# The first cross attention of a decoder as a pipeline over three batches

## The chip, the cores and the metric

One core of a Trainium2 chip runs the whole kernel: two decoder layers on an input of 8 batches of 256 rows by 256 columns. The metric is device time in microseconds from start to end of one execution; the median of three runs of the kernel before is 3400.91 us (3396.31 to 3406.21). PE is TensorE, DVE VectorE, ACT ScalarE, POOL GpSimd; SP issues the DMAs.

## The reference

The decoder has six sublayers, each added to a residual stream x. Only the second is changed, a linear attention over the context (16 heads of 16 columns, batches of 256 queries and 256 keys):

```python
def _focused_feature_map(x, scale):
    x = jax.nn.relu(x) + EPS
    x = x / scale
    x_norm = jnp.linalg.norm(x, axis=-1, keepdims=True)
    xp = x ** FOCUS                      # FOCUS = 3, EPS = 1e-6
    return xp / jnp.linalg.norm(xp, axis=-1, keepdims=True) * x_norm
q = input_q @ Wq + bq                    # input_q = layernorm(x)
k = input_k @ Wk + bk                    # input_k = input_v = ctx_1024
v = input_v @ Wv + bv
q = _focused_feature_map(q, softplus(scale)); k = _focused_feature_map(k, softplus(scale))
# split in heads, then
z = 1.0 / (einsum('bhic,bhc->bhi', q, k.sum(axis=2)) + EPS)
kv = einsum('bhjc,bhjd->bhcd', k, v)
x = x + einsum('bhic,bhcd->bhid', q, kv) * z[..., None]
```

## The kernel before

The residual x (`x_all`), its normalised transpose (`xnT_all`) and an identity matrix stay in SBUF; PSUM is one tensor of 8 banks. The stages (attention, this cross attention, switch attention, attention, cross attention, experts) follow one another, each as a block of one program per engine; the block ends when all its engines have ended, and in front of each stage stands a normalisation with a block of its own (`normalise`, L135 to L198). Within a block the order of an engine's work is its program, written out by hand; engines wait for each other by semaphores that count up.

The changed stage is `linear_attention` (L716). Each engine runs a loop over the 8 batches. In one batch:

- SP (L753) waits until the projections of the batch before are done and loads the batch's normalised input and its context (L755, L756). There is one buffer of each.
- PE projects K, Q and V (L770) into banks 0, 1 and 2 (4 matmuls each; a float32 matmul shows as two records in the trace), after DVE has added the result of the batch before to the residual (`out_taken`).
- DVE adds the biases of K (L834) and Q (L836) into the tile `f`, which holds the two row tiles of Q and the two of K, takes the maximum with 0 and adds EPS (L837), multiplies by the inverse scale (L838), and adds V's bias (L842).
- ACT squares the four row tiles of `f` into `f2` with their sums in `norm2` (L804); DVE multiplies to the cube `f3` (L846); ACT squares that with its sums in `norm6` (L810); DVE takes the reciprocal (L848) and the product with `norm2` (L849), the ratio; ACT takes its root (L813); DVE scales the four row tiles of `f3` with it (L853).
- PE multiplies K by V, with a column of ones for the sum over keys, into bank 3 (L776), and transposes Q into bank 4 (L781). DVE keeps the parts within a head (L858, L859), ACT copies the transposed Q to SBUF (L815), and PE multiplies the two into banks 5 and 6 (L788).
- DVE makes `z` (L864, L865), the quotient `o` (L867), and adds it to the residual (L873).

POOL has no part in this stage. The helper `over_batches` (L100), which the first attention uses already, runs a body with three flags: whether the batch itself (new), the next (ahead) and the one before (old) exist; it is written out for the rounds -1, 0, 7 and 8, and a loop runs rounds 1 to 6. `wait` (L89) leaves a wait out when its value is a constant 0 or less. `alone` (L69) is a wait followed by an increment of a semaphore that nobody waits for.

Of the kernel before, what the change touches and what calls it, by code (L numbers as in the profile page):

```python
# [11 lines left out]
ALU = mybir.AluOpType  # L12
ACT = mybir.ActivationFunctionType
AX = mybir.AxisListType

P = 128
# [699 lines left out]
def linear_attention(nc, norm, x_all, xnT_all, ident, psum, a):  # L716

    with ExitStack() as stack:
# [18 lines left out]
        consts, own_dve, own_setup = s.sem("consts"), s.sem("own_dve"), s.sem("own_setup")  # L737
        projected, taken, features_raw = s.sem("projected"), s.sem("taken"), s.sem("features_raw")
        squared, cubed, sixth, ratio_ready, factor_ready = (
            s.sem(n) for n in ("squared", "cubed", "sixth", "ratio_ready", "factor_ready"))  # L740
        features, kv_summed, kv_ready = s.sem("features"), s.sem("kv_summed"), s.sem("kv_ready")
        q_turned, qT_ready, out_ready, out_taken = (s.sem(n) for n in ("q_turned", "qT_ready", "out_ready", "out_taken"))
        own_act = s.sem("own_act")
# [16 lines left out]
        def _(pe):  # L760
            pe.wait_ge(loaded, 16 * len(loads))
            with pe.Fori(0, B) as b:
                pe.wait_ge(x_here, b * 16 + 16)
                pe.wait_ge(ctx_here, b * 16 + 16)

                pe.wait_ge(out_taken, b)
                for n, (src, weights) in enumerate(((ctxT, wk), (xnT, wq), (ctxT, wv))):
                    for t in range(TT):
                        for c in range(CC):
                            ins = pe.matmul(psum[:, n, t * D:(t + 1) * D], src[:, c, t * P:(t + 1) * P], weights[:, c, :],  # L770
                                            start=(c == 0), stop=(c == CC - 1))
                    ins.then_inc(projected, 1)
                pe.wait_ge(features, b + 1)
                for c in range(CC):
                    for t in range(TT):
                        ins = pe.matmul(psum[:, 3, c * (P + 1):(c + 1) * (P + 1)], f3[:, TT + t, c * P:(c + 1) * P],  # L776
                                        v1[:, t, c, :], start=(t == 0), stop=(t == TT - 1))
                ins.then_inc(kv_summed, 1)
                for c in range(CC):
                    for t in range(TT):  # L780
                        ins = pe.transpose(psum[:, 4, c * T + t * P:c * T + (t + 1) * P], f3[:, t, c * P:(c + 1) * P],  # L781
                                           ident[:])
                ins.then_inc(q_turned, 1)
                pe.wait_ge(kv_ready, b + 1)
                pe.wait_ge(qT_ready, b + 1)
                for t in range(TT):
                    for c in range(CC):
                        ins = pe.matmul(psum[:, 5 + t, c * KVW:(c + 1) * KVW], qT[:, c, t * P:(t + 1) * P], kv[:, c, :],  # L788
                                        start=True, stop=True)
                ins.then_inc(out_ready, 1)  # L790

        @block.scalar
        def _(act):
# [7 lines left out]
            with act.Fori(0, B) as b:  # L801
                act.wait_ge(features_raw, b + 1)
                for i in range(2 * TT):
                    ins = act.activation(f2[:, i, :], f[:, i, :], ACT.Square, accum_out=norm2[:, i:i + 1])  # L804
                ins.then_inc(squared, 1)
                act.wait_ge(cubed, b + 1)

                act.wait_ge(squared, b + 1)
                for i in range(2 * TT):
                    ins = act.activation(f2[:, i, :], f3[:, i, :], ACT.Square, accum_out=norm6[:, i:i + 1])  # L810
                ins.then_inc(sixth, 1)
                act.wait_ge(ratio_ready, b + 1)
                act.activation(factor[:], factor[:], ACT.Sqrt).then_inc(factor_ready, 1)  # L813
                act.wait_ge(q_turned, b + 1)
                act.activation(qT[:], psum[:, 4, :].rearrange("p (c t) -> p c t", c=CC), ACT.Copy).then_inc(qT_ready, 1)  # L815

        @block.vector
        def _(dve):
# [3 lines left out]
            dve.tensor_scalar(scale_e[:], inv_scale[:], CAP, None, ALU.min).then_inc(consts, 1)  # L822
            dve.wait_ge(own_act, 2)
            step.link(dve.tensor_tensor(inv_scale[:], inv_scale[:], scale_e[:], ALU.max))
            step.link(dve.reciprocal(inv_scale[:], inv_scale[:]))
            with dve.Fori(0, B) as b:
                step = Steps(dve, own_dve, b * 9, 9)
                step.wait()

                dve.wait_ge(out_taken, b)  # L830
                dve.wait_ge(projected, b * 3 + 1)
                bias = lambda v: v[:].unsqueeze(1).to_broadcast([P, TT, D])
                tile = lambda n: psum[:, n, :].rearrange("p (t d) -> p t d", t=TT)
                step.did(dve.tensor_tensor(f[:, TT:2 * TT, :], tile(0), bias(bk), ALU.add))  # L834
                dve.wait_ge(projected, b * 3 + 2)
                step.link(dve.tensor_tensor(f[:, 0:TT, :], tile(1), bias(bq), ALU.add))  # L836
                step.link(dve.tensor_scalar(f[:], f[:], 0.0, FOCUS_EPS, ALU.max, ALU.add))  # L837
# [1334 lines left out]
```

## Time and profile before

| | us |
|---|---|
| median of three runs | 3400.91 |
| profiled execution, its time | 3403.3 |
| span of that execution | 3401.4 |
| stage: first DVE instruction (L821) | 980.54 |
| stage: last DVE instruction ends (L873) | 1167.98 |
| first DVE instruction of the next stage (L162) | 1168.34 |
| separate maximum L837, of 1024 elements | 0.694 |
| four scalings L853, together | 1.14 |
| residual sum L873, of 512 elements | 0.693 |

The page divides the span into 40 slices of 85 us and shows tenths: PE busy `6788888888655489999979999999998999968998`, granted clock of PE `8888988899766689999965999999998999968999` (10 tenths are 2.4 GHz). The changed stage lies in slices 11 to 13, counted from 0. Over the whole span PE is busy 86%, DVE 55%, ACT 48%, POOL 20%. Times of instructions are microseconds from the start of the span.

### The profile page before, as it was taken

How to read it: one execution, taken by the hardware profiler on the slowest of the kernel's cores; microseconds unless marked ns; L12 is line 12 of the kernel's file. 1: busy time of each engine (PE TensorE's matmuls, PEld its weight loads, DVE VectorE, ACT ScalarE, POOL GpSimd, SP SyncE). 2: the span in 40 equal slices, each digit the busy share in tenths (PEclk: the TensorE clock that was granted, in tenths of full speed). 3: DMA queues.
4: the chain of work that ended last, by engine and by line, in shares of the span. 5: the costliest groups of instructions: out<-in, count | busy, mean ns of one | idle time of the engine just before them, and what ended most of it. 6: DMA issues, size and time to landing. Idle time of an engine off the chain costs nothing. (4 is left out here: it accounts for less than half of the span.)

```text
span 3401.4 us, 50572 instructions
## 1 busy us (share of the span) xinstructions
PE 2926.5 (86%) x17024; PEld 2085.1 (61%) x17024; DVE 1863.0 (55%) x4064; ACT 1617.8 (48%) x2895; POOL 685.0 (20%) x798
## 2 busy tenths in 40 slices
PE   6788888888655489999979999999998999968998
PEld 3344444444334356776732888888886777747887
DVE  4777877787633456656531444444444544544444
ACT  3887888878721234444511333333333555532221
POOL 1122222222100044444500000000001655620000
PEclk8888988899766689999965999999998999968999
DMA  2000000000010110110110000000002000010000
GB/s 94 4 4 3 3 0 3 3 3 0 1 35 19 54 44 23 23 42 22 21 58 0 4 3 3 3 3 3 3 0 85 4 6 6 3 69 22 6 6 28
DMA packets 88230, 60.88 MB, mean 18 GB/s; under 512 B 54816, under 2 KB 76704, under 8 KB 87648
## 3 DMA queue, kind: packets, MB, share of 16 engines
q1 hardware_dynamic: 88160, 59.99, 5.8%
q8 instruction: 39, 0.64, 0.1%
q14 instruction: 31, 0.25, 0.0%
HBM read 41.10 MB, written 8.39 MB: 15 GB/s over the span
## 5 line engine op out<-in xcount | busy, mean ns | idle before, releaser
L1772 POOL TENSOR_SCALAR x_weights<-x_weights,x_sums 128x256 f32<-128x256 f32 x256 | 231.7, 924 | 1066.5 <-DVE x_sums L1809 1066.5
L670 DVE SCALAR_TENSOR_TENSOR a_w<-a_w,a_sinks 128x384 f32<-128x384 f32 x512 | 332.7, 714 | 31.5 <-ACT a_w L505 31.5
L1074 POOL TENSOR_SCALAR f_weights<-f_weights,f_sums 128x256 f32<-128x256 f32 x256 | 232.2, 924 | 271.2 <-DVE f_sums L1304 271.2
L1501 ACT ACTIVATE a_weights<-psum,a_negmax 128x1024 f32<-128x1024 f32 x128 | 142.5, 1114 | 293.1 <-DVE a_negmax L1541 293.1
L484 ACT ACTIVATE a_e<-psum 128x1024 f32<-128x1024 f32 x192 | 195.4, 1018 | 158.0 <-PE psum L343 118.9
L1475 PE MATMUL psum<-a_v,a_turned_w 128*128 128x128 f32 x2048 | 248.3, 275 | 0.0
L1475 PEld LDWEIGHTS psum<-a_v,a_turned_w 128*128 128x128 f32 x2048 | 238.1, 192 | 0.0
L1541 DVE TENSOR_REDUCE a_negmax<-psum 128x1 f32<-128x1024 f32 x128 | 156.7, 1224 | 124.9 <-PE psum L123 124.0
L1232 ACT ACTIVATE f_weights<-psum,f_negmax 128x256 f32<-128x256 f32 x256 | 117.8, 472 | 215.1 <-DVE f_negmax L1298 215.1
L340 PE MATMUL psum<-a_qT,a_kT_half 32*128 32x512 f32 x512 | 166.5, 730 | 60.6 <-DVE a_w L685 48.7
L685 DVE SCALAR_TENSOR_TENSOR a_w<-a_e,psum 128x512 f32<-128x512 f32 x256 | 162.6, 675 | 96.1 <-ACT a_e L486 86.6
L486 ACT ACTIVATE a_e<-a_e 128x1024 f32<-128x1024 f32 x192 | 202.9, 1057 | 6.1
L1742 ACT ACTIVATE x_weights<-x_masked_s,x_negmax 128x256 f32<-128x256 f32 x256 | 126.9, 496 | 147.1 <-DVE x_negmax L1805 147.0
L505 ACT ACTIVATE a_w<-a_w 128x1536 f32<-128x1536 f32 x128 | 179.4, 1472 | 0.4
L1466 PE MATMUL psum<-all_ident,a_weights 128*128 128x128 f32 x1024 | 133.8, 274 | 9.5 <-ACT a_weights L1501 9.5
L1466 PEld LDWEIGHTS psum<-all_ident,a_weights 128*128 128x128 f32 x1024 | 118.3, 140 | 29.9 <-ACT a_weights L1501 14.2
L370 PE MATMUL psum<-a_w,a_v 128*32 128x512 f32 (+1 forms) x1024 | 114.6, 575 | 19.8 <-DVE a_w L670 19.8
L188 PE MATMUL psum<-all_ident,ln_xn 128*128 128x128 f32 x192 | 53.4, 434 | 82.3 <-DVE ln_xn L177 82.3
L121 PE MATMUL psum<-a_kT_hi,a_qT_hi 128*128 128x512 f32 x256 | 110.7, 432 | 11.3 <-DVE a_qT_lo L1535 11.3
L340 PEld LDWEIGHTS psum<-a_qT,a_kT_half 32*128 32x128 f32 x512 | 44.1, 210 | 113.5 <-DVE a_w L685 59.8
L343 PEld LDWEIGHTS psum<-a_future,a_ident_r 128*128 128x128 f32 x256 | 42.5, 209 | 113.5 <-issue 113.5
L566 POOL TENSOR_TENSOR a_ctxn<-a_ctx,a_vnull 128x256 f32<-128x256 f32 x64 | 45.1, 725 | 330.2 <-DVE a_ctx L640 330.2
(304 smaller groups left out, 6820.1 us busy)
## 6 DMA issues: line engine op xcount, KB each, us to landing
a_xnT<-all_xnT_all SPq DMA_DIRECT2D x16, 256.0 KB, 2.3
x_ctxT<-in_x_ctxT SPq DMA_DIRECT2D x16, 256.0 KB, 2.7
f_xnT<-all_xnT_all SPq DMA_DIRECT2D x16, 256.0 KB, 2.3
f_pv_rows<-f_pv SPq DMA_DIRECT2D x8, 512.0 KB, 3.1
f_pv_groups<-f_pv_rows SPq DMA_DIRECT2D x8, 512.0 KB
f_w<-in_f_w SPq DMA_DIRECT2D x2, 2048.0 KB, 10.3
all_x_all<-in_x SPq DMA_DIRECT2D x1, 2048.0 KB, 8.4
a_wq<-in_a_wq SPq DMA_DIRECT2D x2, 1024.0 KB, 9.2
```

The costliest lines, as they stand in the source:

```text
L340: pe.matmul(psum[:, 2 * x + h, :], kT_half[rows[h], step % 2, g, 0:P], qT[rows[h], g, 2 * x:2 * x + 2, :], start=True, stop=False)
L484: act.activation(e[:, x, :], psS[x], ACT.Exp).then_inc(exp_done, 1)
L486: act.activation(e[:, x, :], e[:, x, :], ACT.Ln, bias=1.0).then_inc(ln_done, 1)
L505: act.activation(wu, wu, ACT.Silu, scale=SILU_SCALE).then_inc(silu_done, 1)
L670: ins = dve.scalar_tensor_tensor(part, part, sinks[:, col:col + 1], part, ALU.is_ge, ALU.mult)
L685: ins = dve.scalar_tensor_tensor(wu[:, h, 2 * x:2 * x + 2, 0:T], by_branch(e[:, x, :]), CAP, by_branch(psS[x]), ALU.min, ALU.max)
L1074: ins = pool.tensor_scalar(w, w, sums[:, k, h, t:t + 1], None, ALU.mult)
L1466: ins = pe.transpose(psum[:, 4 + half, j * P:(j + 1) * P], weights[k % 2][:, lo:lo + P], ident[:])
L1475: ins = pe.matmul(psum[:, 6 + k % 2, 0:AD], turned_w[:, k % 2, j * P:(j + 1) * P], v[:, j, h * AD:(h + 1) * AD], start=(j == 0), stop=(j = ...
L1501: act.activation(weights[k % 2][:], psum[:, 2 * (k % 2):2 * (k % 2) + 2, :].rearrange("p a n -> p (a n)"), ACT.Exp, bias=negmax[:, k:k + 1 ...
L1541: dve.tensor_reduce(negmax[:, k:k + 1], psum[:, 2 * (k % 2):2 * (k % 2) + 2, :].rearrange("p a n -> p (a n)"), AX.X, ALU.max, negate=True) ...
L1772: ins = pool.tensor_scalar(w, w, sums[:, k, h, t:t + 1], None, ALU.mult)
```

## The change

The stage becomes a pipeline by `over_batches`. In round b, PE first projects batch b+1 and then does the KV product, the transposes and the output of batch b. DVE makes the cube of batch b, then `z` and `o` of batch b-1, K's bias of b+1, the ratio of b, Q's bias and the features of b+1, the masked KV of b, the copy of the transposed Q of b (which ACT did), and V's bias of b+1. ACT takes the sixth powers and the root of b, scales the four row tiles of b (which DVE did), K first, with a semaphore for K and one for Q, and squares the features of b+1. POOL adds `o` of batch b-1 to the residual (which DVE did). EPS is added to the biases once in the setup, and maximum and inverse scale become one instruction. SP's program is unchanged; no buffer is added. The diff from PE's program on; lines taken out are left out here, they stand in the function above:

```diff
...
         @block.tensor
         def _(pe):
             pe.wait_ge(loaded, 16 * len(loads))
...
+            def project(b):
                 pe.wait_ge(x_here, b * 16 + 16)
                 pe.wait_ge(ctx_here, b * 16 + 16)
...
+                wait(pe, features_raw, b)
                 for n, (src, weights) in enumerate(((ctxT, wk), (xnT, wq), (ctxT, wv))):
+                    if n == 2:
+                        wait(pe, v_taken, b)
                     for t in range(TT):
                         for c in range(CC):
                             ins = pe.matmul(psum[:, n, t * D:(t + 1) * D], src[:, c, t * P:(t + 1) * P], weights[:, c, :],
                                             start=(c == 0), stop=(c == CC - 1))
                     ins.then_inc(projected, 1)
...
+            def body(b, new, ahead, old):
+                if ahead:
+                    project(b + 1)
+                if new:
+                    pe.wait_ge(k_scaled, b + 1)
+                    pe.wait_ge(v_taken, b + 1)
+                    wait(pe, kv_ready, b)
+                    for c in range(CC):
+                        for t in range(TT):
+                            ins = pe.matmul(psum[:, 3, c * (P + 1):(c + 1) * (P + 1)], f3[:, TT + t, c * P:(c + 1) * P],
+                                            v1[:, t, c, :], start=(t == 0), stop=(t == TT - 1))
+                    ins.then_inc(kv_summed, 1)
+                    pe.wait_ge(q_scaled, b + 1)
+                    wait(pe, qT_ready, b)
+                    for c in range(CC):
+                        for t in range(TT):
+                            ins = pe.transpose(psum[:, 4, c * T + t * P:c * T + (t + 1) * P], f3[:, t, c * P:(c + 1) * P],
+                                               ident[:])
+                    ins.then_inc(q_turned, 1)
+                    pe.wait_ge(kv_ready, b + 1)
+                    pe.wait_ge(qT_ready, b + 1)
+                    wait(pe, o_made, b)
                     for t in range(TT):
...
+                        for c in range(CC):
+                            ins = pe.matmul(psum[:, 5 + t, c * KVW:(c + 1) * KVW], qT[:, c, t * P:(t + 1) * P], kv[:, c, :],
+                                            start=True, stop=True)
+                    ins.then_inc(out_ready, 1)
+            over_batches(pe, body)
         @block.scalar
         def _(act):
...
             step.link(act.activation(scale_e[:], scale_e[:], ACT.Exp))
             step.link(act.activation(scale_e[:], scale_e[:], ACT.Ln, bias=1.0))
             act.preload_act_table_set("sqrt_and_others")
...
+            def body(b, new, ahead, old):
+                if new:
+                    act.wait_ge(squared, b + 1)
+                    act.wait_ge(cubed, b + 1)
+                    for i in range(2 * TT):
+                        ins = act.activation(f2[:, i, :], f3[:, i, :], ACT.Square, accum_out=norm6[:, i:i + 1])
+                    ins.then_inc(sixth, 1)
+                    act.wait_ge(ratio_ready, b + 1)
+                    act.activation(factor[:], factor[:], ACT.Sqrt).then_inc(factor_ready, 1)
+                    act.wait_ge(factor_ready, b + 1)
+                    for i, done in ((TT, None), (TT + 1, k_scaled), (0, None), (1, q_scaled)):
+                        ins = act.activation(f3[:, i, :], f3[:, i, :], ACT.Copy, scale=factor[:, i:i + 1])
+                        if done:
+                            ins.then_inc(done, 1)
+                if ahead:
+                    act.wait_ge(features_raw, b + 2)
+                    for i in range(2 * TT):
+                        ins = act.activation(f2[:, i, :], f[:, i, :], ACT.Square, accum_out=norm2[:, i:i + 1])
+                    ins.then_inc(squared, 1)
+            over_batches(act, body)
+        @block.gpsimd
+        def _(pool):
+            def body(b, new, ahead, old):
+                if old:
+                    alone(pool, o_made, b, passed)
+                    x_b = x_all[:, bass.ds((b - 1) * TT, TT), :]
+                    pool.tensor_tensor(x_b, x_b, o[:], ALU.add).then_inc(x_added, 1)
+            over_batches(pool, body)
         @block.vector
         def _(dve):
...
             step = Steps(dve, own_setup)
             step.did(dve.memset(v1[:, :, :, P:P + 1], 1.0))
             dve.tensor_scalar(scale_e[:], inv_scale[:], CAP, None, ALU.min).then_inc(consts, 1)
+            step.did(dve.tensor_scalar(bk[:], bk[:], FOCUS_EPS, None, ALU.add))
+            step.did(dve.tensor_scalar(bq[:], bq[:], FOCUS_EPS, None, ALU.add))
             dve.wait_ge(own_act, 2)
             step.link(dve.tensor_tensor(inv_scale[:], inv_scale[:], scale_e[:], ALU.max))
             step.link(dve.reciprocal(inv_scale[:], inv_scale[:]))
...
+            bias = lambda v: v[:].unsqueeze(1).to_broadcast([P, TT, D])
+            tile = lambda n: psum[:, n, :].rearrange("p (t d) -> p t d", t=TT)
+            def body(b, new, ahead, old):
+                if new:
+                    dve.wait_ge(squared, b + 1)
+                    wait(dve, q_turned, b)
+                    dve.tensor_tensor(f3[:], f2[:], f[:], ALU.mult).then_inc(cubed, 1)
+                if old:
+                    dve.wait_ge(out_ready, b)
+                    outs = psum[:, 5:5 + TT, 0:CC * KVW].rearrange("p t (c n) -> p t c n", c=CC)
+                    dve.tensor_scalar(z[:], outs[:, :, :, P:KVW], FOCUS_EPS, None, ALU.add).then_inc(z_made, 1)
+                    dve.wait_ge(z_made, b)
+                    dve.reciprocal(z[:], z[:]).then_inc(z_inverted, 1)
+                    dve.wait_ge(z_inverted, b)
+                    wait(dve, x_added, b - 1)
+                    for t in range(TT):
+                        ins = dve.tensor_tensor(o[:, t, :].rearrange("p (c h d) -> p c h d", c=CC, h=HEADS_IN_CHUNK),
+                                                outs[:, t, :, 0:P].rearrange("p c (h d) -> p c h d", h=HEADS_IN_CHUNK),
+                                                z[:, t].unsqueeze(3).to_broadcast([P, CC, HEADS_IN_CHUNK, P // HEADS_IN_CHUNK]),
+                                                ALU.mult)
+                    ins.then_inc(o_made, 1)
+                if ahead:
+                    wait(dve, cubed, b + 1)
+                    dve.wait_ge(projected, b * 3 + 4)
+                    dve.tensor_tensor(f[:, TT:2 * TT, :], tile(0), bias(bk), ALU.add).then_inc(raw_f, 1)
+                if new:
+                    dve.wait_ge(sixth, b + 1)
+                    dve.reciprocal(factor[:], norm6[:]).then_inc(inverted, 1)
+                    dve.wait_ge(inverted, b + 1)
+                    dve.tensor_tensor(factor[:], factor[:], norm2[:], ALU.mult).then_inc(ratio_ready, 1)
+                if ahead:
+                    dve.wait_ge(projected, b * 3 + 5)
+                    dve.tensor_tensor(f[:, 0:TT, :], tile(1), bias(bq), ALU.add).then_inc(raw_f, 1)
+                    dve.wait_ge(raw_f, b * 2 + 4)
+                    dve.scalar_tensor_tensor(f[:], f[:], FOCUS_EPS, inv_scale[:].unsqueeze(1).to_broadcast([P, 2 * TT, D]),
+                                             ALU.max, ALU.mult).then_inc(features_raw, 1)
+                if new:
+                    dve.wait_ge(kv_summed, b + 1)
+                    wait(dve, out_ready, b)
+                    for c in range(CC):
+                        lo = c * (P + 1)
+                        dve.tensor_tensor(kv[:, c, 0:P], psum[:, 3, lo:lo + P], same_head[:], ALU.mult)
+                        ins = dve.tensor_tensor(kv[:, c, P:KVW], psum[:, 3, lo + P:lo + P + 1].to_broadcast([P, HEADS_IN_CHUNK]),
+                                                head_mask[:], ALU.mult)
+                    ins.then_inc(kv_ready, 1)
+                    dve.wait_ge(q_turned, b + 1)
+                    dve.tensor_copy(qT[:], psum[:, 4, :].rearrange("p (c t) -> p c t", c=CC)).then_inc(qT_ready, 1)
+                if ahead:
+                    dve.wait_ge(projected, b * 3 + 6)
+                    for t in range(TT):
+                        ins = dve.tensor_tensor(v1[:, t, :, 0:P], psum[:, 2, t * D:(t + 1) * D].rearrange("p (c d) -> p c d", c=CC),
+                                                bv[:].rearrange("p (c d) -> p c d", c=CC), ALU.add)
+                    ins.then_inc(v_taken, 1)
+            over_batches(dve, body)
```

## Rows read from the trace of the kernel before

**Rows 1.** Busy time by stretch: its length, then each engine's, clock, DMA share, GB/s
```profile
core 0: us, PE busy (x) PEld busy (x) DVE busy (x) ACT busy (x) POOL busy (x), PEclk, DMA share, GB/s
980.54:1167.98 187.44, 97.75 (x352) 80.09 (x352) 76.83 (x180) 37.09 (x148) 0.00 (x0) 0.68 0.07 22
...
1053.15:1076.00 22.85, 12.07 (x44) 10.00 (x45) 9.29 (x22) 4.21 (x18) 0.00 (x0) 0.65 0.08 23
1260.00:1500.00 240.00, 224.58 (x1790) 163.79 (x1791) 147.73 (x225) 112.08 (x321) 112.27 (x124) 1.00 0.12 29
1800.00:1850.00 50.00, 50.00 (x51) 12.48 (x50) 5.53 (x8) 4.78 (x8) 0.00 (x0) 0.50 0.00 0
```
**Rows 2.** Waits, 980 to 1168: who for whom, us in total, times, longest
```profile
ACT x_f L804 <- DVE x_f L838: 97.9, 8, 13.5
```
**Rows 3.** Timeline, 1053 to 1076: start, us, engine, line; in brackets idle time before
```profile
1053.15 3.53 PE L770 MATMUL psum<-x_wk,x_ctxT 128*128 128x256 f32 x8 [2.40 <-DVE all_x_all L873]
1056.52 1.89 PE L770 MATMUL psum<-x_wq,x_xnT 128*128 128x256 f32 x8
1058.25 1.89 PE L770 MATMUL psum<-x_wv,x_ctxT 128*128 128x256 f32 x8
...
1060.27 0.50 SPq L755 DMA_DIRECT2D x_xnT<-all_xnT_all  x1
1060.97 0.43 SPq L756 DMA_DIRECT2D x_ctxT<-in_x_ctxT  x1
...
1061.16 0.42 ACT L804 ACTIVATE x_f<-x_f 128x256 f32<-128x256 f32 x1 [11.71 <-DVE x_f L838]
...
1067.73 2.09 PE L776 MATMUL psum<-x_v,x_f 128*128 128x129 f32 x8 [7.59 <-DVE x_f L853]
...
1069.61 1.06 PE L781 MATMUL psum<-all_ident,x_f 128*128 128x128 f32 x4
...
1075.16 0.69 DVE L873 TENSOR_TENSOR all_x_all<-all_x_all,x_o 128x512 f32 x1 [0.15 <-DVE x_o L867]
...
1076.00 3.75 PE L770 MATMUL psum<-x_wk,x_ctxT 128*128 128x256 f32 x8 [2.40 <-DVE all_x_all L873]
```
**Rows 4.** DVE by line and form, whole span: busy us, mean ns, idle before
```profile
L689 DVE SCALAR_TENSOR_TENSOR a_w<-a_e,psum 128x1024 f32<-128x1024 f32 x64 | 77.2, 1206 | 32.3 <-ACT a_e L486 32.3
...
L1275 DVE COPY f_vT<-psum 128x512 f32<-128x512 f32 x32 | 32.2, 1044 | 39.0 <-PE psum L1118 38.3
...
L846 DVE TENSOR_TENSOR x_f<-x_f 128x1024 f32<-128x1024 f32 x8 | 9.8, 1226 | 8.8 <-ACT x_f L804 8.8
...
L1525 DVE COPY a_v<-psum 128x512 f32<-128x512 f32 x8 | 5.5, 691 | 57.9 <-PE psum L1429 57.9
```
**Rows 5.** POOL by line and form, whole span
```profile
L584 POOL TENSOR_TENSOR all_x_all<-all_x_all,a_bo 128x512 f32 x6 | 7.7, 1277 | 0.0
```
**Rows 6.** Timeline, start of the stage
```profile
981.43 0.42 SPq L756 DMA_DIRECT2D x_ctxT<-in_x_ctxT  x1
...
984.18 3.75 PE L770 MATMUL psum<-x_wk,x_ctxT 128*128 128x256 f32 x8 [4.50 <-DMA x_ctxT<-in_x_ctxT]
```
**Rows 7.** Timeline of PE: output of the first two batches, next K projection
```profile
1002.83 2.15 PE L788 MATMUL psum<-x_kv,x_qT 128*128 128x136 f32 x8 [0.78 <-ACT x_qT L815]
...
1026.38 1.16 PE L788 MATMUL psum<-x_kv,x_qT 128*128 128x136 f32 x8 [0.78 <-ACT x_qT L815]
1029.95 3.75 PE L770 MATMUL psum<-x_wk,x_ctxT 128*128 128x256 f32 x8 [2.40 <-DVE all_x_all L873]
```
**Rows 8.** Timeline of PE in the next stage
```profile
1277.59 1.08 PE L1118 MATMUL psum<-f_mix_blocks,f_pv_groups 128*64 128x256 f32 x8 [1.76 <-DMA f_mix_blocks<-f_mix_rows]
...
1280.53 1.99 PE L1098 MATMUL psum<-all_xnT_all,f_wk 128*128 x8
...
1291.21 0.65 PE L1124 MATMUL psum<-all_ident,f_vT 128*128 128x128 f32 x4 [0.92 <-DVE f_vT L1275]
```
**Rows 9.** Timeline in the first attention: DVE alone, then beside POOL
```profile
873.53 4.84 DVE L670 SCALAR_TENSOR_TENSOR a_w<-a_w,a_sinks 128x384 f32<-128x384 f32 x9
...
232.53 3.66 DVE L670 SCALAR_TENSOR_TENSOR a_w<-a_w,a_sinks 128x384 f32<-128x384 f32 x4
232.81 1.46 POOL L578 TENSOR_TENSOR a_kT<-a_kT,a_ksq 128x512 f32<-128x512 f32 x1 [21.52 <-ACT a_ksq L497]
```

More of the change, by code:

```diff
@@ L736, in linear_attention @@
         loaded, x_here, ctx_here = s.sem("loaded"), s.sem("x_here"), s.sem("ctx_here")
[L737 to L743, printed above, removed]
+        consts, own_setup, own_act, passed = s.sem("consts"), s.sem("own_setup"), s.sem("own_act"), s.sem("passed")
+        projected, v_taken, raw_f, features_raw = s.sem("projected"), s.sem("v_taken"), s.sem("raw_f"), s.sem("features_raw")
+        squared, cubed, sixth, inverted, ratio_ready, factor_ready = (
+            s.sem(n) for n in ("squared", "cubed", "sixth", "inverted", "ratio_ready", "factor_ready"))
+        k_scaled, q_scaled, kv_summed, kv_ready = (s.sem(n) for n in ("k_scaled", "q_scaled", "kv_summed", "kv_ready"))
+        q_turned, qT_ready, out_ready, z_made, z_inverted, o_made, x_added = (
+            s.sem(n) for n in ("q_turned", "qT_ready", "out_ready", "z_made", "z_inverted", "o_made", "x_added"))
         loads = [(wq[:], chunked(a["wq"])), (wk[:], chunked(a["wk"])), (wv[:], chunked(a["wv"])),
@@ L761, in _ @@
             pe.wait_ge(loaded, 16 * len(loads))
-            with pe.Fori(0, B) as b:
+            def project(b):
                 pe.wait_ge(x_here, b * 16 + 16)
                 pe.wait_ge(ctx_here, b * 16 + 16)
-                pe.wait_ge(out_taken, b)
+                wait(pe, features_raw, b)
                 for n, (src, weights) in enumerate(((ctxT, wk), (xnT, wq), (ctxT, wv))):
+                    if n == 2:
+                        wait(pe, v_taken, b)
                     for t in range(TT):
@@ L772, in _ @@
                     ins.then_inc(projected, 1)
-                pe.wait_ge(features, b + 1)
-                for c in range(CC):
-                    for t in range(TT):
[L776 to L790, printed above, removed]
+            def body(b, new, ahead, old):
[20 more added lines that the diff above has]
+                    wait(pe, o_made, b)
+                    for t in range(TT):
+                        for c in range(CC):
+                            ins = pe.matmul(psum[:, 5 + t, c * KVW:(c + 1) * KVW], qT[:, c, t * P:(t + 1) * P], kv[:, c, :],
+                                            start=True, stop=True)
+                    ins.then_inc(out_ready, 1)
@@ L800, in _ @@
             act.preload_act_table_set("sqrt_and_others")
[L801 to L815, printed above, removed]
+            def body(b, new, ahead, old):
[17 more added lines that the diff above has]
+                    ins.then_inc(squared, 1)
```

48 lines of the change are left out of this document (removed).

## The prediction

> **What bounds the kernel now.** I read the page's slices first (in the table above): PE is busy 80 to 100% nearly everywhere, with a dip in slices 11 to 13, where the changed stage lies. The table by stretch [rows 1] gives the stage, from its first DVE instruction to its last (980.54 to 1167.98): 187.44 us, PE busy 52%, DVE 41%, ACT 20%, POOL nothing, clock 0.68. No engine is its bound, so it must be a chain of waits. The table of waits has ACT first, 97.9 us for features [rows 2]. The timeline of one batch [rows 3] is that chain link by link: projections from 1053.15, biases, squares from 1061.16, cube, sixth powers, ratio, scaling, KV product at 1067.73, transposes, output, residual sum ending at 1075.85, and the next batch's first matmul at 1076.00. A batch costs 22.85 us; the eight starts run from 984.18 to 1145.26, 23.0 apart. Nothing outside this stage is edited, and stages follow one another through a common end, so what the stage saves the kernel saves.
>
> **Who does what after the change.** DVE is busy 9.29 us in a batch [rows 1]. It loses the maximum (0.69), the four scalings (1.14) and the residual sum (0.69; all three in the table above) and gains the copy of qT. For that copy the DVE copies of 512 elements from PSUM stand [rows 4]: 0.69 the usual one, 1.04 the slowest; 0.60 is what ACT takes for it now. I take 0.69, the same source layout. The maximum and the multiplication become one scalar_tensor_tensor of 1024 elements: a two-input one of 1024 takes 1.23, a scalar_tensor_tensor of 1024 with a PSUM operand 1.21 [rows 4]; I take 1.23, what the multiplication alone takes now. So 9.29 - 0.69 - 1.14 - 0.69 + 0.69 = 7.46, and with a dozen gaps of 0.04 between instructions 7.9 us a round. ACT: eight squares in two groups of 1.71, the root's 0.2 and four scalings at 0.40 (as its 256 element activation, [rows 3]): 5.2 us. POOL: one sum of 1.28 us [rows 5], on nobody's path except at the very end. Two additions to the biases (0.29 each, by the 256 element tensor_scalar of the setup) run while DVE waits 2.21 us for ACT's exponential: nothing; without that cover 0.6 us once.
>
> **PE per round.** A projection follows the one before by 1.73 us at the high clock (1056.52 to 1058.25, [rows 3]) and by 3.5 at the low one (3.75 less the tail, [rows 6]), its result out 0.16 to 0.2 later. Output: 1.16 us high, 2.15 low [rows 7]. The KV product was never at the high clock here (2.09 all eight times, one in [rows 3]): bounds 1.04 and 2.09; by its size against the output's I take 1.12. Four transposes: 1.06 low [rows 3], 0.65 high [rows 8].
>
> **The round, with K0 the start of the K projection of batch b+1, high clock.** K is out at K0+1.93, Q 3.66, V 5.35. PE takes KV of batch b at 5.19 if K is scaled; out at 6.31, transposes 6.73. DVE: masks 6.35 to 6.97, qT 7.00 to 7.69. The output matmuls start 0.14 later (as K after the residual sum in [rows 3]), at 7.83, are issued by 8.76 and out at 9.00. PE's chain gives 8.76. The other chain is the input load, which has one buffer, and SP waits for the V projection: V out 5.35, first issue 0.13 later, the context's 0.70 after (1060.27, 1060.97, [rows 3]), 2.75 from there to the first matmul (981.43 to 984.18, [rows 6]): 8.93. The load is last, by 0.2: **a round is 8.94 us** instead of 23.0.
> Does DVE keep up? The V bias ends at 8.48, the next batch's cube at 9.74, z and o at 11.14, which is 2.20 in the next round; K bias 2.92 (its data came at 1.93). The sixth powers are ready at 2.55. With the ratio ahead of the Q bias it ends at 3.32, instead of standing behind Q's arrival at 3.66 and that bias of 0.69; root 3.56, K scaled 4.45, Q scaled 5.3. PE wants them at 5.19 and 6.07: slack 0.7. Q bias 3.70 to 4.39, features to 5.65, squares 5.71 to 7.42, and the cube can't start before 8.48 anyway. DVE idles 0.7 us for KV. With the ratio behind the Q bias K would be scaled at 5.5, 0.3 late: that ordering is worth some 2 us in all.
>
> **POOL beside DVE.** The residual sum runs from about 2.5 to 3.75 in the round, over K bias and ratio. The trace shows what POOL does to a DVE instruction with two SBUF inputs: nine of L670 take 4.84 us alone, 0.54 each, and four take 3.66 beside POOL's multiplication of 1.46 [rows 9], 1.5 more, POOL's whole time. K bias has a PSUM operand; the small ratio multiplication may be held until 3.75, ends then at 3.9, and K is scaled at 5.0, inside the slack: price 0. With no slack, 0.5 us a round, 4 us.
> The Trainium skill (GPSIMD Engine Reference, its table of specifications) says that GpSimd's SBUF interfaces are shared with VectorE and contend with instructions that have two SBUF inputs; rows 9 agree. By that rule with the features instruction caught too, for POOL's whole 1.28 us, the stage would be some 4 us longer beyond the slack of 0.7; POOL has ended before it starts.
>
> **Start and end.** Up to the V projection of batch 0, out at 991.51, nothing changes. Then the load of batch 1: 991.64, 992.34, landed 995.10. PE was idle 3.6 us; K projections behind 2.4 us of idleness were at the low clock all 7 times (two stand in [rows 3, 7]), so K(1) takes 3.5; Q(1), between 1.73 and 3.5, 2.25 as the mean of the eight batches; V(1) out at 1002.74. K(2) starts 3.59 later, 1006.33 (KV and output of batch 0 fit before it). K(7) is five rounds on: 1051.03. Output 6 is out at 1060.03. The last batch has no cover: cube 1060.8, z and o 1062.2, ratio 1062.9, K scaled 1064.0, KV at the low clock 1066.2, masks, transposes, qT 1067.8, output 1070.1, z and o 1071.5, POOL's sum 1073.0. The next stage begins 0.3 later, as now. **Stage end 1073.0 against 1167.98: 95.0 us less.** The profiled execution took 3403.3 (span 3401.4), so 3308.3; it was 2.4 above the median 3400.9, so 3306 for the median.
>
> **Rivals.** *The clock doesn't hold.* The sum takes the high clock from K(2) on. For it: projections of this shape go high within a batch [rows 3]; the next stage has an idle time of 1.76 us with the matmuls behind it at the high clock [rows 8], and 1.00 over 240 us at 94% busy [rows 1]; the new round idles 1.1 us before the output and 0.2 before K. Against: 2.4 us of idleness always lost it, and from 1800 to 1850 PE is 100% busy at 0.50 [rows 1], so busy is not enough. Wholly at the low clock a round is 10.5 + 1.9 + 0.2 + 1.5 + 2.0 = 16.1, 7.2 more, over six rounds 43 us: 3349. One round in four: 3317.
> The Trainium skill (TensorE: Matmul & The Clock Gate, "A second HAM failure mode: psum-queue depth-cycling") describes a kernel that idled briefly between groups of matmuls and swung between the two clocks. By that rule about half of the rounds would be slow, some 3328. The gap of 1.76 us, longer than the new ones, speaks against it here.
> *One batch's chain stays the round.* If the cube of b+1 could not start before o of b, a round would be the chain from squares to o (1061.16 to 1075.0, [rows 3]) and the biases and features ahead of it, 15.8 us: +41 us, 3347. The code lets the cube wait only for its squares and the transposes before, so I give this little.
> *DVE becomes the round.* If the copy from PSUM takes 1.04, POOL holds the features instruction (1.28) and the ratio (0.5): 7.9 + 0.35 + 1.28 + 0.5 = 10.0, one us a round, 3313.
> *Slower than before.* A later stage could begin at another point of the clock's own rhythm and stay low though busy, as 1800 to 1850 does. If the next stage did so in 1260 to 1500, its 224.6 us of PE work [rows 1] would double: +225 - 95, 3531. It decides from 95 us of such work. Against: the three timed runs lie within 10 us, and the next stage starts from an idle PE either way.
>
> **How the numbers follow.** The sum as written: 70%, its own range 3299 to 3313 (the median moves 5 us either way, 0.2 us a round is 1 us). Clock partly or wholly low: 18%. DVE round: 6%. Chain stays: 4%. Slower: 2%. The range 3298 to 3334 leaves out the full low clock, the unbroken chain and the slow case. About 0.3% can be told from no change: faster 0.97, same 0.01, slower 0.02.
>
> **What would show it.** K projections 8.9 us apart from the third on, Q 1.73 after K; the load as the releaser of K by 0.2 us; eight POOL sums of 1.3 us; DVE waiting 0.7 us a round for KV; PE busy near 90% and the clock near 1 in the rounds. Wrong if that clock is under 0.9, if rounds are over 9.5 us, or if the time outside the stage moves by over 5 us.

## The result and the profile after

The changed kernel takes 3310.89 us (median of 4 runs, 3309.46 to 3313.78) against 3399.34 (4 runs, 3396.31 to 3406.21) of the kernel before: ratio 0.9735, 95% interval 0.9721 to 0.9750. Forecast were 3306 us, range 3298 to 3334, faster with 0.97. The profiled execution took 3313.78 us (span 3312.0).

Busy time by stretch in the changed kernel, the answer to [rows 1]: the whole stage, and the five rounds from the third K projection on.

```profile
core 0: us, PE busy (x) PEld busy (x) DVE busy (x) ACT busy (x) POOL busy (x), PEclk, DMA share, GB/s
979.60:1073.80 94.20, 69.47 (x352) 59.62 (x352) 61.13 (x142) 45.97 (x172) 10.12 (x8) 0.90 0.14 45
1006.75:1052.67 45.92, 39.56 (x221) 34.57 (x221) 35.88 (x86) 26.62 (x105) 6.35 (x5) 1.00 0.18 57
```

The stage lasts 94.2 us instead of 187.4. PE's busy time fell from 97.75 to 69.47 us for the same 352 recorded matmuls: the clock rose from 0.68 to 0.90, and stands at 1.00 in the rounds. DVE fell from 76.83 to 61.13, ACT took on 8.9 and POOL 10.1. In the table of waits, ACT's wait for features, 97.9 us in [rows 2], is now 13.7; what POOL waits is POOL's own leisure:

```profile
POOL all_x_all L849 <- DVE x_o L883: 116.5, 8, 61.4
ACT x_f L825 <- DVE x_f L871: 15.7, 8, 2.0
ACT x_f L837 <- DVE x_f L902: 13.7, 8, 7.8
```

One round of the timeline of all engines (start, us, engine, line), the answer to [rows 3]:

```profile
1025.34 1.97 PE L773 MATMUL psum<-x_wk,x_ctxT 128*128 128x256 f32 x8 [0.45 <-issue]
...
1026.96 1.27 POOL L849 TENSOR_TENSOR all_x_all<-all_x_all,x_o 128x512 f32 x1 [8.00 <-DVE x_o L883]
...
1027.34 0.69 DVE L892 TENSOR_TENSOR x_f<-psum,x_bk 128x512 f32<-128x512 f32 x1 [0.64 <-PE psum L773]
...
1028.15 0.16 DVE L897 TENSOR_TENSOR x_factor<-x_factor,x_norm 128x4 f32<-128x4 f32 x1
...
1028.58 1.70 ACT L831 ACTIVATE x_f<-x_f,x_factor 128x256 f32<-128x256 f32 x4
...
1029.79 1.23 DVE L902 SCALAR_TENSOR_TENSOR x_f<-x_f,x_inv_scale 128x1024 f32<-128x1024 f32 x1
...
1030.59 1.05 PE L787 MATMUL psum<-x_v,x_f 128*128 128x129 f32 x8
...
1031.48 0.60 PE L795 MATMUL psum<-all_ident,x_f 128*128 128x128 f32 x4
1031.58 0.43 SPq L756 DMA_DIRECT2D x_ctxT<-in_x_ctxT  x1
...
1032.23 0.68 DVE L915 COPY x_qT<-psum 128x512 f32<-128x512 f32 x1
...
1033.02 1.17 PE L804 MATMUL psum<-x_kv,x_qT 128*128 128x136 f32 x8 [0.94 <-DVE x_kv L911]
...
1034.53 1.97 PE L773 MATMUL psum<-x_wk,x_ctxT 128*128 128x256 f32 x8 [0.35 <-issue]
```

From K to K it is 9.19 us here; the six K projections from the third on start 9.29, 9.30, 9.19, 9.09 and 9.05 apart, 9.18 on average. PE is idle twice in a round, 0.94 before the output and 0.35 before K, the second time with nothing named as releaser ("issue"). The context is issued at 1031.58 and K starts 2.95 later. Whether the load is what PE waits for there, the row doesn't say. The trace has the landings of these loads as well (five of them, us from issue to landing):

```profile
DMA to landing us min/median/max: 2.7/2.9/3.0
```

The one issued at 1031.58 lands at 1034.44, and K starts 0.09 later; in all six rounds K starts 0.09 or 0.10 after the landing. x_early below moves the load and tests this.

The stage itself, from its first DVE instruction to the next normalisation, went from 187.80 to 94.58 us, 93.2 less, while the medians are 88.5 apart.

### The profile page after: what moved, and what is told of

Read it like the earlier page. It is cut to its first block and busy times, and to the rows that moved or that the text cites. A ratio compares the mean times of both kernels' runs of the same rounds, so it can differ in the third digit from the quotient of the medians.

```text
span 3312.0 us, 50542 instructions
## 1 busy us (share of the span) xinstructions
PE 2904.0 (88%) x17024; PEld 2068.3 (62%) x17024; DVE 1849.1 (56%) x4026; ACT 1628.1 (49%) x2919; POOL 695.1 (21%) x806
## 5 line engine op out<-in xcount | busy, mean ns | idle before, releaser
L1791 ACT ACTIVATE x_weights<-x_masked_s,x_negmax 128x256 f32<-128x256 f32 x256 | 126.9, 496 | 145.4 <-DVE x_negmax L1854 145.3
```

## The experiments

All stage lengths here are from the stage's first DVE instruction to the first one of the next normalisation, in the one profiled execution of each kernel: 187.8 for the kernel before, 94.6 for the changed one. The medians stand beside those of the kernel before on the same chip.

**as_is.** The changed kernel again.

> The changed kernel once more, for the scatter of its stages. My theory: the changed stage is the same to 0.3 us (94.6 us from its first DVE instruction to the next normalisation, K projections 9.05 to 9.30 apart), and what the kernel gives back outside it (the gain was 93.2 in the stage and 88.5 in the medians) is the scatter of the other stages, which follows the clock: the switch attention, 555.9 before and 562.1 after, will come out elsewhere between these. Rival: the later stages have really become 4 to 5 us longer by the change; then the switch attention is at 562 again and the second cross attention at 452.

Measured: 3305.1 against 3395.15, ratio 0.9736 (0.9723 to 0.9749). Stage 93.9, K projections 9.12 to 9.29 apart. The stage is 0.7 shorter and not the same to 0.3: here the second batch's Q projection ran at the high clock (25.4 us from the stage's start to the third K projection instead of 27.1) and the last output at the low one (22.5 from the last K projection to the next normalisation instead of 21.5). Normalisation to normalisation, the switch attention took 559.3 us, the second cross attention 450.1. Over all twelve profiles the first lies between 553.5 and 562.1, and the second at 450 to 453 or at 458; its 562.1 in the changed kernel's profile was the longest of all.

**before_again.** The kernel before again, one run.

> The kernel before once more, for the scatter of its later stages. If the 5 us that the total gave back are scatter, the switch attention comes out between 553 and 562 us and the second cross attention at 450 or 458 here too; the changed stage, 187.8 from its first DVE instruction to the next normalisation, is the same to 1 us.

Measured: one run of 3394.1, stage 187.8, switch attention 557.4 (555.9 in the first profile), second cross attention 450.1 (457.8). So the same code differs by 8 us in one later stage between two executions; of the changed kernel's later stages one, the switch attention of 562.1, lies outside what the other profiles scatter (553.5 to 559.3), and it was 559.3 when the same kernel ran again. Over the changed kernel, its repetition and the eight variants below, the gain in the medians falls short of the gain in the stage by 2.1 us on average, from 6.2 short (sum_on_dve) to 5.0 beyond (k_pool_late). The interval of the ratio, 0.0015 either way, is 5 us; the stage's 93.2 lies within 88.5 plus 5. That the change itself costs the later stages something of a few us is not excluded by this, but nothing shows it.

**x_early.** The input (`load_x`) is issued behind the Q projection, the context (`load_ctx`) behind V, with the same two transfers as before.

```diff
-                sp.wait_ge(projected, b * 3)
...
+            load_x(0)
+            load_ctx(0)
+            for i in range(B - 1):
+                sp.wait_ge(projected, i * 3 + 2)
+                load_x(i + 1)
+                sp.wait_ge(projected, i * 3 + 3)
+                load_ctx(i + 1)
```

> The normalised input of the next batch is loaded once Q is projected, the context once V is, instead of both after V. Theory (the input load ends last in a round): the input's issue, 0.70 us, leaves the chain; K projections 8.65 apart instead of 9.18, the second one 0.7 sooner, stage 91.3 us instead of 94.6. Rival (PE, KV, masks, qT, output is the chain and the load only arrives with it): rounds stay at 9.1 to 9.2, stage 93.9.

Measured: 3301.79 against 3395.15, ratio 0.9721 (0.9702 to 0.9741), stage 90.1. In the whole time the interval overlaps that of as_is, so the gain is shown in the stage only. The rounds are 8.61 us each, to 0.01:

```profile
1011.65 1.17 PE L813 MATMUL psum<-x_kv,x_qT 128*128 128x136 f32 x8 [0.93 <-DVE x_kv L920]
1012.66 1.89 PE L782 MATMUL psum<-x_wk,x_ctxT 128*128 128x256 f32 x8
...
1020.26 1.17 PE L813 MATMUL psum<-x_kv,x_qT 128*128 128x136 f32 x8 [0.93 <-DVE x_kv L920]
1021.26 1.89 PE L782 MATMUL psum<-x_wk,x_ctxT 128*128 128x256 f32 x8
```

K now follows the output without idle time, 0.45 to 0.79 after the context has landed. The load was last in the changed kernel, by 0.57 us a round, and behind it stands PE's own chain of 8.6. Of the 4.4 us that the stage lost the rounds are 2.9; 0.8 is the second K projection's earlier load, and 1.6 is mostly the high clock of the second batch's Q projection, which as_is had by chance too; the end is 0.9 longer, with the last output at the low clock.

The shorter round has changed something else, without a cost here: the ratio's multiplication of 4 elements now stands beside POOL's sum and takes 0.80 instead of 0.16.

```profile
1014.90 1.27 POOL L858 TENSOR_TENSOR all_x_all<-all_x_all,x_o 128x512 f32 x1 [7.38 <-DVE x_o L892]
1015.39 0.80 DVE L906 TENSOR_TENSOR x_factor<-x_factor,x_norm 128x4 f32<-128x4 f32 x1
```

**preload.** The loads leave the loop: the context of all batches comes with the weights; PE's rounds are written out, since it now reads a part of a larger tile by a constant.

```diff
-        xnT, ctxT = s.sb("xnT", [P, CC, T]), s.sb("ctxT", [P, CC, T])
+        ctxT = s.sb("ctxT", [P, B, CC, T])
...
-                for n, (src, weights) in enumerate(((ctxT, wk), (xnT, wq), (ctxT, wv))):
+                for n, (src, weights) in enumerate(((ctxT, wk), (xnT_all, wq), (ctxT, wv))):
```

> No load inside the loop: the context of all batches is loaded during the normalisation before, PE reads it and the normalised input in place, its rounds written out. Theory: rounds 8.6, set by PE's own chain (7.7 from K to the output's start, 0.93 its matmuls); the first K projection 4 us sooner, the second right behind V of batch 0 and at the high clock: 3 us of waiting and 3 us of low clock less. Stage 81 to 83 us, kernel 12 us faster than the changed one. Rival (DVE is what a round really costs): rounds stay above 9.0, stage 85 or more.

Measured: 3291.61 against 3395.15, ratio 0.9696 (0.9683 to 0.9709), stage 83.1, rounds 8.60 to 8.61. The rounds are those of x_early; the 7 us more are the start, where the first K projection doesn't wait for its load and comes 4.4 us sooner, and the second comes 7.8 us after it instead of the 10.0 of x_early, at the high clock (1.99 instead of 3.65). The normalisation in front, where the context is loaded now, has not become longer: 20.8 us, as in the kernel before. The ratio's multiplication takes 0.77 to 0.80 beside POOL's sum here too, and KV follows V without idle time.

**k_first.** preload, and PE's order changed.

```diff
                 if ahead:
-                    project(b + 1)
+                    project(b + 1, (0, 1, 2) if b < 0 else (1, 2))
+                    if b < 0:
+                        project(1, (0,))
...
+                    if b + 2 < B:
+                        project(b + 2, (0,))
                     pe.wait_ge(kv_ready, b + 1)
                     pe.wait_ge(qT_ready, b + 1)
```

> The kernel without loads in the loop, and PE projects K of the batch after next while DVE masks KV and copies qT, ahead of the output product. Theory: PE's idle time of 0.93 a round is filled, and DVE's own work becomes the round: 7.2 us of work and its gaps, 7.6 to 8.0 between K projections, stage 77 us. Rival (the chain from KV over masks, qT and output to z of the next round closes through DVE, and filling PE only delays the output): rounds stay at 8.6, stage as without the reordering.

Measured: 3289.17 against 3395.15, ratio 0.9693 (0.9680 to 0.9706), stage 82.2, rounds 8.45. Neither expectation: the idle time before the output is gone, yet only 0.15 a round came of it. The timeline shows why:

```profile
1015.02 1.27 POOL L846 TENSOR_TENSOR all_x_all<-all_x_all,x_o 128x512 f32 x1 [7.17 <-DVE x_o L880]
1015.26 0.17 DVE L892 RECIPROCAL x_factor<-x_norm 128x4 f32<-128x4 f32 x1
1015.46 0.84 DVE L894 TENSOR_TENSOR x_factor<-x_factor,x_norm 128x4 f32<-128x4 f32 x1
...
1016.34 0.21 ACT L825 ACTIVATE x_factor<-x_factor 128x4 f32<-128x4 f32 x1 [1.23 <-DVE x_factor L894]
...
1017.53 1.16 PE L781 MATMUL psum<-x_v,x_f 128*128 128x129 f32 x8 [0.74 <-ACT x_f L828]
```

The ratio's multiplication of 4 elements, with two SBUF inputs, takes 0.84 us and ends at 1016.30, when POOL's sum ends (1016.29). PE then waits 0.74 for K's scaling. The hold itself isn't new, x_early and preload have it. What is new is that K's projection, 1.7 us, no longer stands between the output and KV, so that PE is ready for KV before K is scaled: the slack that hid the hold is gone.

**k_pool_late.** k_first with POOL's sum moved.

```diff
                     alone(pool, o_made, b, passed)
+                    if ahead:
+                        alone(pool, features_raw, b + 2, passed)
+                    elif new:
+                        alone(pool, ratio_ready, b + 1, passed)
```

> k_first, where the ratio's multiplication stands 0.84 us beside POOL's sum instead of 0.16 and K's scaling waits for it; here POOL starts its sum only after the features of the next batch (in the last round, after the ratio). Theory (POOL holds a DVE instruction with two SBUF inputs, and in k_first that is on the chain): the ratio's multiplication takes 0.16 again, rounds 7.7 to 7.9 instead of 8.45, the stage 4 us shorter than k_first's 82.2. Rival (DVE's own work is the round): rounds stay above 8.2, stage 81 or more.

Measured: stage 77.5, rounds 7.76 to 7.77, 3289.1 against 3404.32, ratio 0.9671 (0.9651 to 0.9691):

```profile
1019.24 1.28 POOL L850 TENSOR_TENSOR all_x_all<-all_x_all,x_o 128x512 f32 x1 [6.49 <-DVE x_f L903]
...
1019.74 1.89 PE L765 MATMUL psum<-x_wk,x_ctxT 128*128 128x256 f32 x8
...
1024.68 0.16 DVE L898 TENSOR_TENSOR x_factor<-x_factor,x_norm 128x4 f32<-128x4 f32 x1
...
1027.51 1.89 PE L765 MATMUL psum<-x_wk,x_ctxT 128*128 128x256 f32 x8
```

The multiplication takes 0.16 again, and a round lost exactly its 0.68. The sum now lies over instructions with a PSUM operand. What sets this round is PE itself, busy 38.52 us of the five rounds' 38.83; DVE still idles 0.7 us in each:

```profile
996.45:1035.28 38.83, 38.52 (x223) 33.68 (x222) 35.10 (x87) 26.30 (x107) 5.61 (x5) 1.00 0.00 1
```

This kernel has the lowest ratio of all; its interval and k_first's overlap, so in the whole time the last step is not shown, only in the stage.

**split_only.** The kernel before, its loop over single batches kept, with the new division of the work: besides the lines shown the scalings are ACT's, the copy of qT is DVE's and the sum POOL's, by the lines of the changed kernel.

```diff
-                step.link(dve.tensor_scalar(f[:], f[:], 0.0, FOCUS_EPS, ALU.max, ALU.add))
-                dve.tensor_tensor(f[:], f[:], inv_scale[:].unsqueeze(1).to_broadcast([P, 2 * TT, D]), ALU.mult)\
-                   .then_inc(features_raw, 1)
+                dve.scalar_tensor_tensor(f[:], f[:], FOCUS_EPS, inv_scale[:].unsqueeze(1).to_broadcast([P, 2 * TT, D]),
+                                         ALU.max, ALU.mult).then_inc(features_raw, 1)
...
-                for i in range(2 * TT):
-                    ins = dve.tensor_scalar(f3[:, i, :], f3[:, i, :], factor[:, i:i + 1], None, ALU.mult)
```

> The kernel before with the new division of the work (one instruction for maximum and scale, scalings on ACT, qT copy on DVE, sum on POOL), but one batch after the other as before. Theory: the chain of a batch loses 0.73 (maximum), 0.3 (K alone is scaled before KV) and 0.84 (sum), and gains 0.1 (qT): 1.8 us a batch, 14 of the 93 us; stage 173 to 174 us from its first DVE instruction to the next normalisation, and the overlap of batches is the other 79. If PE's idle time before a K projection, now 1.6 us instead of 2.4, keeps the clock, K takes 1.8 us less too and the stage is 160. Rival: the division is what brings most, stage under 140.

Measured: 3383.22 against 3397.29, ratio 0.9954 (0.9939 to 0.9969), stage 170.0: 17.8 us for the division, 75.4 for the overlap. A batch takes 20.1 to 21.3 us. The seven K projections behind 1.55 us of idle time are still at the low clock (3.29 to 3.65); in each batch there are 6.6 us of idleness ahead of KV besides.

**late_load.** The load of batch b+2 waits for the output of batch b.

```diff
+                sp.wait_ge(projected, i * 3 + 6)
+                sp.wait_ge(out_ready, i + 1)
+                load(i + 2)
```

> The changed kernel, but the inputs of batch b+2 are loaded only once the output of batch b is made, so that PE is idle 4.1 us in every round. Tells what the clock is worth. If idleness of 4 us loses the high clock each time (my theory): K projections 14.5 to 15.5 apart (9.2, the later load 3.6, the K and Q projections 2.3 longer), stage 128 to 132 us. If the high clock holds with the same work: 12.8 apart, stage 116.

Measured: 3335.94 against 3397.29, ratio 0.9830 (0.9805 to 0.9854), stage 126.9, K projections 13.8 to 15.7 apart, 14.7 on average from the third on:

```profile
1039.28 3.59 PE L780 MATMUL psum<-x_wk,x_ctxT 128*128 128x256 f32 x8 [3.51 <-issue]
1042.71 1.89 PE L780 MATMUL psum<-x_wq,x_xnT 128*128 128x256 f32 x8
...
1067.18 3.75 PE L780 MATMUL psum<-x_wk,x_ctxT 128*128 128x256 f32 x8 [3.54 <-issue]
1070.72 3.17 PE L780 MATMUL psum<-x_wq,x_xnT 128*128 128x256 f32 x8
```

Idle times of 3.5 to 3.9 us lose the high clock every time: K takes 3.4 to 3.75 instead of 1.9, Q 1.9 to 3.2. Over these five rounds the clock is 0.80. Of the 5.5 us more a round 3.3 are the longer wait (3.6 on average instead of 0.3) and the other 2.2 the clock. The overlap thus holds the clock as well as hiding the chain.

**ratio_behind.** On DVE, Q's bias stands ahead of the ratio of the norms; the features stay behind both.

```diff
+                if ahead:
+                    dve.wait_ge(projected, b * 3 + 5)
+                    dve.tensor_tensor(f[:, 0:TT, :], tile(1), bias(bq), ALU.add).then_inc(raw_f, 1)
                 if new:
                     dve.wait_ge(sixth, b + 1)
...
                 if ahead:
-                    dve.wait_ge(projected, b * 3 + 5)
-                    dve.tensor_tensor(f[:, 0:TT, :], tile(1), bias(bq), ALU.add).then_inc(raw_f, 1)
```

> The changed kernel with the ratio of the norms after the bias of Q on DVE. By the prediction K is scaled 0.7 us after PE could start KV, against a load that has 0.5 us to spare: rounds 9.3 instead of 9.2, stage 1 to 2 us longer (95.6 to 96.6). Rival (the order of these two is worth a whole delay of Q, 0.7 us and more a round): rounds 9.9, stage 99.

Measured: 3310.02 against 3397.29, ratio 0.9742 (0.9724 to 0.9761), stage 98.2, rounds 9.47:

```profile
1036.60 1.89 PE L773 MATMUL psum<-x_wk,x_ctxT 128*128 128x256 f32 x8
...
1040.25 0.69 DVE L895 TENSOR_TENSOR x_f<-psum,x_bq 128x512 f32<-128x512 f32 x1 [1.03 <-PE psum L773]
...
1041.50 1.70 ACT L831 ACTIVATE x_f<-x_f,x_factor 128x256 f32<-128x256 f32 x4
...
1042.54 1.15 PE L787 MATMUL psum<-x_v,x_f 128*128 128x129 f32 x8 [0.60 <-ACT x_f L831]
...
1046.07 0.38 PE L773 MATMUL psum<-x_wk,x_ctxT 128*128 128x256 f32 x1
```

KV starts 5.94 after K, 0.69 later than in the changed kernel (1030.59 against 1025.34), and the load, which has landed by then, no longer matters. The delay is that of my expectation, 0.7; what the round gives up against the load is 0.3, not 0.1. The stage is 3.6 to 4.4 us longer than in the two executions of the changed kernel, but 1 to 1.7 of that is the clock of single instructions, which differs between those two as well. Compared where the clock is the same, the order is worth 2.7: 0.5 up to the third K projection (against the changed kernel), 1.4 in the five rounds, and 0.8 behind the last K projection (against as_is). The rival's 0.7 a round isn't there.

**sum_on_dve.** The residual sum back on DVE.

```diff
                     ins.then_inc(o_made, 1)
+                    dve.wait_ge(o_made, b)
+                    x_b = x_all[:, bass.ds((b - 1) * TT, TT), :] if not isinstance(b, int) else x_all[:, (b - 1) * TT:b * TT, :]
+                    dve.tensor_tensor(x_b, x_b, o[:], ALU.add).then_inc(x_added, 1)
+                    dve.wait_ge(x_added, b)
...
-        @block.gpsimd
```

> The changed kernel with the residual sum on DVE again, POOL idle. Theory (DVE has room, POOL's sum holds nothing that matters): rounds as in the changed kernel, 9.05 to 9.3, stage 94 to 95. Rival 1 (DVE is nearly the round): rounds 0.3 longer or more, stage 96 to 97. Rival 2 (POOL beside DVE costs time in every round): stage 91 to 93.

Measured: 3309.58 against 3397.29, ratio 0.9742 (0.9722 to 0.9762), stage 93.9, rounds 9.05 to 9.16 but the first, 9.63, where SP's issue took 1.07 instead of 0.43. As in the changed kernel: DVE had room for the sum, and POOL's taking it over brings nothing in the rounds. At the stage's end, which no round covers, it costs: from the last K projection to the next normalisation 20.7 us here and 21.5 in the changed kernel, both with the last output at the high clock.

## Why the prediction was right, and where it was off

- *The bound.* A chain of waits through one batch at a time, no engine: right. The division of the work alone gives 17.8 us, the overlap 75.4 (split_only). With rounds of 9.18 the rival in which one batch's chain stays the round, 15.8, is out.
- *The round, 8.94 us.* Measured 9.18 on average. The mechanism was right: the input load ends last, and PE's own chain stands behind it (x_early: 0.57 us less a round). Its size was off on both sides. Of the load: from K to the context's issue 6.24 instead of 6.18 (1025.34 to 1031.58), from there to the next K 2.92 on average over six rounds, between 2.79 and 3.05, where I had the one 2.75 of the first load in [rows 6]. PE's chain I had at 8.76, measured 8.61 (x_early): the output starts 7.60 after K instead of 7.83, mostly because KV takes 1.05 instead of 1.12 and the copy of qT starts at 6.82 instead of 7.00, and the next K starts 1.00 behind it instead of 0.93. So the margin is 0.57, not 0.2.
- *The clock.* Right: 1.00 in all rounds, with PE busy 86% of them (the sign named was near 90%). The rival took 18%; late_load shows that it was a real one, since with 3.5 us and more of idle time a round the high clock is lost every time. The new gaps, 0.94 and 0.15 to 0.45, don't lose it. Which gap would, between these and 3.5, is open; split_only's 1.55 lost it, but behind a longer one in the same batch.
The Trainium skill (TensorE: Matmul & The Clock Gate, "A second HAM failure mode: psum-queue depth-cycling") has a kernel whose brief idle times between groups of matmuls made it swing between the two clocks; it gives no share, and the half of the rounds in the prediction was my own. The trace doesn't agree here: the changed kernel idles twice a round and stays at 1.00.
- *DVE keeps up.* Right. The features instruction takes 1.23, the copy of qT 0.68, and DVE's order fits; it idles 2.2 us in a round of the changed kernel, 0.67 of that for KV, where 0.7 was forecast. With the loads gone and PE's gap filled the round becomes 7.77 (k_pool_late), less than the 7.9 that I worked out for DVE's own, and PE sets it; so k_first's theory that DVE would become the round was wrong.
- *The order of ratio and Q bias.* Right in kind, somewhat small in size: 2 us forecast, 2.7 measured at the same clock (ratio_behind). There is a slip in my working: Q's bias ends at 4.39, ratio, root and two scalings take 0.40, 0.24 and 0.89 more, which is 5.9 and not the 5.5 I wrote; KV starts at 5.94 there.
- *POOL beside DVE, price 0.* Right in the rounds. The sum runs earlier than forecast, from 1.6 to 2.9 in the round shown and not from 2.5 to 3.75, so that it lies mostly over K's bias, and the ratio's multiplication takes 0.16 to 0.38. That the slack would have covered a full hold, as the prediction says, x_early shows: 0.77 to 0.80 in every round and no wait for it. In the last round, which has no K bias in front of it, the changed kernel has 0.70:

```profile
1063.51 1.26 POOL L849 TENSOR_TENSOR all_x_all<-all_x_all,x_o 128x512 f32<-128x512 f32 x1 [7.70 <-DVE x_o L883]
1063.87 0.18 DVE L895 RECIPROCAL x_factor<-x_norm 128x4 f32<-128x4 f32 x1 [0.55 <-ACT x_f L825]
1064.08 0.70 DVE L897 TENSOR_TENSOR x_factor<-x_factor,x_norm 128x4 f32<-128x4 f32 x1
```

It ends at 1064.78, with POOL's sum at 1064.77. There it is on the chain, since the last batch has no cover. In k_first the same hold is on the chain of every round.
- *Start and end.* From the stage's start to K(2) 25.8 forecast, 27.1 measured: Q(1) was at the low clock throughout (2.99 to the next, where I took the mean, 2.25), and the first load landed 3.35 after its issue instead of 2.66. K(0) starts 4.4 us after the stage's start instead of 3.6; in all seven profiles of kernels other than the one before that load within the stage it is 4.1 to 4.4, and in the two of the kernel before 3.6 and 3.7. Why stays open. From K(7) to the end 22.0 forecast, 21.1 measured: the last output was at the high clock (1.17) there, and at the low one (2.15) when the same kernel ran again.
- *The sum.* Stage 92.8 us to the next normalisation forecast, 94.6 measured: 1.2 from the rounds, 1.4 from the start, less 0.8 at the end. For the whole kernel I forecast 95 less; the medians say 88.5 and, in the second comparison, 90.1, with 5 either way. So of the 5 us by which the forecast of 3306 was off, less than 2 are the stage. That nothing outside the stage moves, the step on which the forecast of the whole kernel rests, is not proved to better than a few us. The sign I had named for being wrong, 5 us outside the stage, is too fine: 93.2 less 88.5 is 4.7, and the kernel before alone differs by 8 in one stage between two executions.
- *The slow rival* didn't come about: no later stage is longer by more than 7 us than in the kernel before, in any of the profiles. Its example was badly chosen. The stretch at 0.50 though PE is busy 100% is there in all twelve profiles, from 50 to 125 us behind the start of the same normalisation, whenever that comes; so it belongs to that work (float32 matmuls of 64x512), not to a moment.

## What to carry to other kernels

Where every engine is half idle and each waits for the next, overlapping batches pays twice: it hides the chain, and it closes the idle time that costs PE its clock. Work out the new round for each chain that closes in it, the single-buffered load among them, with the durations of several rows and not of one; the second longest chain says what removing the first is worth. When a round is shortened, look again at what now runs beside what: an instruction on another engine, as POOL's sum here, can come to hold one that the chain needs, and this stays unseen as long as there is slack (x_early) and costs once the slack is used (k_first).

## What I had not expected of the hardware

POOL's sum holds a DVE instruction with two SBUF inputs even if that has only 4 elements: up to 0.86 us instead of 0.16, and in each of the held cases (changed kernel, as_is, x_early, preload, k_first) until 0.02 us after the sum's end. DVE instructions with one PSUM operand beside the same sum (K's bias 0.68 to 0.69, KV's masks and the copy of qT in k_pool_late 0.28 and 0.68), and the reciprocal of 4 elements with its one input (0.17), keep their time. The prediction had allowed for the hold; [rows 9] had shown it for instructions of 384 elements only, and as a sum over several.
The Trainium skill (GPSIMD Engine Reference, its table of specifications) speaks of contention for shared SBUF interfaces between GpSimd and VectorE instructions with two SBUF inputs; the runs agree, and the contention is seen here as a wait for the end of POOL's instruction.
